# Second layer's attention: products over 64 instead of 49 rows of the query and key tiles, the spare rows zeroed

## What is computed

```python
xn = _layernorm(x, axis=-1)
x = x + _L0_attn_ref(xn, ...) + _L0_ffn_ref(xn, ...)
xn = _layernorm(x, axis=-1)
x = x + _L1_attn_ref(xn, ...) + _L1_ffn_ref(xn, ...)
```

```python
q = rope(heads(x @ W_q.T + b_q))
k = rope(heads(x @ W_k.T + b_k))
v = heads(x @ W_v.T + b_v)
scores = jnp.einsum('bhtd,bhsd->bhts', q, k)
probs = jax.nn.softmax((scores + mask) / jnp.sqrt(jnp.float32(dh)), axis=-1)
out = jnp.einsum('bhts,bhsd->bhtd', probs, v)
out = out.transpose(0, 2, 1, 3).reshape(b, t, d)
return out @ W_o.T + b_o
```

## Time and profile before

| | us |
|---|---|
| median of 3 runs | 2048.22 |
| lowest, highest | 2047.69, 2049.31 |
| the profiled execution | 2053.99 |
| its span, first to last instruction | 2052.1 |
| PE busy in it | 1683.1 (82%) |
| DVE busy | 1229.1 (60%) |
| ACT busy | 901.6 (44%) |
| mean granted clock of PE | 0.891 |

### The profile page before, as it was taken

The page is one execution under the profiler, slowest core; times in us unless marked ns, Lnnn a source line. Parts: engine busy times, 40 slices in busy tenths (PEclk is TensorE's granted clock), DMA queues, the critical chain, the costliest instruction groups (busy, mean ns, idle before and its releaser), DMA issues. The chain is left out here.

```text
span 2052.1 us, 35695 instructions
## 1 busy us (share of the span) xinstructions
PE 1683.1 (82%) x13083; PEld 838.5 (41%) x13083; DVE 1229.1 (60%) x2140; ACT 901.6 (44%) x1457; POOL 768.6 (37%) x423
## 2 busy tenths in 40 slices
PE   2777798798989988899899972459988889898988
PEld 2455354353544535454353432236633333323333
DVE  5422876758675675766766506811357766676573
ACT  0112265364554635546454540213235655455455
POOL 1502745556475663755657671710035000000000
PEclk9998699899998999999999985679979988798688
DMA  4122200000000000000000001233310000000000
GB/s 155 52 81 85 44 12 11 7 22 7 23 12 13 17 10 21 12 18 12 12 19 7 17 6 57 86 105 103 93 41 23 21 27 27 28 2 27 27 1 21
DMA packets 59157, 69.96 MB, mean 34 GB/s; under 512 B 13274, under 2 KB 42862, under 8 KB 58094
## 3 DMA queue, kind: packets, MB, share of 16 engines
q1 hardware_dynamic: 54894, 59.31, 9.3%
q0 software_dynamic: 4096, 8.40, 1.5%
HBM read 43.48 MB, written 19.53 MB: 31 GB/s over the span
## 5 line engine op out<-in xcount | busy, mean ns | idle before, releaser
L1480 POOL TENSOR_TENSOR a_prob_sum<-a_prob_sum,a_prob 128x1024 f32<-128x1024 f32 (+2 forms) x224 | 499.4, 2230 | 236.4 <-ACT a_prob L1428 215.5
L1428 ACT ACTIVATE a_prob<-a_st,a_table 128x512 f32<-128x512 f32 (+3 forms) x640 | 352.7, 626 | 355.3 <-PE a_st L1306 218.1
L1918 DVE TENSOR_REDUCE a_maxima<-a_mx 128x1 f32<-128x512 f32 (+3 forms) x640 | 351.5, 604 | 148.1 <-PE a_mx L1906 107.7
L1526 DVE TENSOR_REDUCE a_maxima<-a_ring 128x16 f32<-128x512 f32 (+3 forms) x640 | 352.8, 600 | 128.9 <-PE a_ring L1238 101.5
L2175 ACT ACTIVATE a_prob<-a_st 128x1024 f32<-128x1024 f32 (+1 forms) x320 | 271.5, 899 | 228.7 <-PE a_st L2075 130.1
L1333 PE MATMUL a_ot<-a_prob,a_values 128*64 128x512 f32 (+3 forms) x1280 | 287.8, 568 | 0.0
L1238 PE MATMUL a_ring<-a_k_hi,a_q_hi 64*128 64x512 f16 (+3 forms) x640 | 165.3, 374 | 92.0 <-DVE a_maxima L1526 69.2
L1906 PE MATMUL a_mx<-a_ks,a_qs 49*128 49x512 bf16 (+3 forms) x640 | 181.5, 393 | 43.1 <-DVE a_maxima L1918 41.7
L2091 PE MATMUL a_ot<-a_prob,a_values 128*32 128x512 f32 (+3 forms) x1280 | 184.7, 633 | 0.0
L1306 PE MATMUL a_st<-a_q_hi,a_k_hi 64*128 64x512 f16 (+4 forms) x704 | 135.1, 339 | 0.0
L2075 PE MATMUL a_st<-a_qs,a_ks 49*128 49x512 bf16 (+3 forms) x640 | 129.9, 401 | 6.1 <-issue 2.4
(11 more groups left out here) (249 smaller groups left out, 2681.8 us busy)
## 6 DMA issues: line engine op xcount, KB each, us to landing
a_rden<-rden_wide SPq DMA_DIRECT2D x64, 128.0 KB, 2.9
f_w<-in_w SPq DMA_DIRECT2D x28, 256.0 KB, 2.8
expert_in<-zeros SPq DMA_DIRECT2D x5, 1024.0 KB, 9.8
f_rows<-expert_in SPq DMA_DIRECT2D x16, 256.0 KB, 3.3
a_values<-values_all SPq DMA_DIRECT2D x8, 512.0 KB
expert_out<-f_result SPq DMA_DIRECT2D x16, 256.0 KB, 2.4
shared_w<-in_w SPq DMA_DIRECT2D x12, 256.0 KB, 3.0
parts<-p_part_t SPq DMA_DIRECT2D x6, 512.0 KB, 2.7
```

The lines of the kernel that those rows point to most:

```text
L1428: e = act.activation(prob[:, s % NPROB, a, c0:QW], ps_st[s % 2][:, a, c0:QW], ACT.Exp, bias=table[x][:, a, at:at + 1])
L1480: pool.tensor_tensor(into[:, :, c0:QW], into[:, :, c0:QW], here[:, :, c0:QW], ALU.add).then_inc(added, 2 if r == TPQ - 2 else 1)
L1526: dve.reduce_max(maxima[:, qt // TPQ, a, qt % TPQ, at:at + count], bank[:, 0:hi - lo].rearrange("p (w k) -> p w k", k=WINDOW), AX_X).then_ ...
L1918: dve.reduce_max(own.maxima[:, qt // TPQ, a, qt % TPQ, n:n + 1], bank[:, 0:hi - lo], AX_X).then_inc(done, 1)
```

## The change

`ROWS1` becomes 64, so that both products (`scores` and `max_pair1`) run over all 64 rows of a half. So that the 15 rows beyond the data hold zeros, `set_ones1` clears each of the two tiles whole before it writes the ones: two memsets over 128 partitions and, behind each, a wait of the engine for its own memset. It is called once on DVE (buffer 0) and once on POOL (buffer 1). The loads, the masks, the order of the work and the data rows stay as they are.

```diff
-ROWS1 = PRODUCTS1 + 1 + 2 * DH1
+ROWS1 = 64
...
+    own.cleared = [ctx.enter_context(nc.semaphore(f"a1_cleared{x}")) for x in range(2)]
...
 def set_ones1(eng, own, x):
 
     ones_twice = float(np.array([0x3F803F80], np.uint32).view(np.float32)[0])
+    for n, tile in enumerate((own.qs[x], own.ks[x])):
+        eng.memset(tile[:, :].bitcast(F32), 0.0).then_inc(own.cleared[x], 1)
+        eng.wait_ge(own.cleared[x], n + 1)
     for a in range(2):
```

## The result

The changed kernel takes 2016.66 us (median of 4 runs, 2006.47 to 2020.33) against 2047.95 us (4 runs, 2044.33 to 2049.31): ratio 0.984, 95% interval 0.980 to 0.988, 31 us less. Measured again beside later kernels it came out at 0.980 (0.975 to 0.986). Now and then a run is disturbed; one that lies more than 1.5% above the quickest run of its kernel is left out of the ratios and the mean clocks. The forecast was 2049.3 us with a range down to 2044.5. The sign that the prediction named for this, a clock of 0.88 or more there, is plain with 0.94.

A forecast was written before the change was run, and what follows sets the result against it. PE was taken to bound the second attention at half clock, PE with DVE at full. The terms 0 + 0 + 1.1 + 0 = +1.1 us on the median 2048.22 gave 2049.3 us, range 2044.5 to 2056.

The forecast's parts named there:

- The sign that the prediction named for this: Last 527 us: a granted clock of 0.88 or more would prove the forecast wrong and Rival one right.
- The views and the bound: Second attention, 527 us: PE alone paces it at half clock (169 us), DVE and PE together at full clock.
- Part one: Scores and maxima products of the second attention: 64 rows for 49 cost 0 and gain 0; bound 8 ns a product.
- Part two: PE's clock in the second attention: set by recent busy time, so 64 rows change nothing, +0 us.
- Part three: Start of the second layer's experts: two more DVE memsets delay SP's loads and PE, +1.1 us, bounds 0 to 3.0.
- rival two: Second attention's group turns: the shifted start brings one more long dip, 6.1 us, giving 2055.4 us; chance 0.09.
- Part four: Second layer's experts: two more POOL memsets of 0.97 us each, cost 0, hidden; without cover 1.9 us.
- Rival one: Second attention: wider rows raise PE's clock; half the time at half clock saved, 30 us, gives 2019 us; chance 0.12.

## Why the prediction was wrong

**The views and the bound: right.** PE at half clock was the bound of the stage. The price of a microsecond at half was put at 0.36 us from two slots. The change gave 42.1 us for 117 us, or 0.36; the 33-row kernel lost 149.7 us (685.3 - 535.6) for 610 - 174 = 436 us more at half, or 0.34. Nothing was mis-sized here.

**Part one, the cost of a row: right.** The 216/376 ns stayed, and the pairs still stand 0.22 us apart at full clock and 0.43 at half. The 8 ns a product that the range allowed for weren't there.

**Part two, the clock: this step failed.** It read the earlier trace rows well up to a point: a PE busy for 13.46 of 13.65 us at half clock means that busy time isn't what the clock goes by. It was then talked out of the consequence by one stretch of the first layer, where products of 64 rows also stayed at half for 13.65 us. That stretch shows only that 64 rows are not always enough; PE had waited in it (12.06 busy of 13.65). It doesn't show that 64 rows don't do more than 49, which was the question. A fair comparison needs the same work at two row counts, and no trace of before held that. So "0 for this part" had no row behind it, and the 0.12 for the rival leaned on that one stretch. The runs showed in its place: 33, 49, 56 and 64 rows give clocks of 0.56, 0.82 to 0.86, 0.91 and 0.93 to 0.94 in the last stage, and the change took PE's time at half clock in the attention from 174 to 57 us, worth 42 us. The rule that was weighed there, from the Trainium skill ("TensorE: Matmul & The Clock Gate", the section on the HAM clock gate), says that recent busy time sets the clock. If busy is read as the share of time that PE's records cover, the 33-row trace is at odds with it: PE was busy for 271.87 of 279.89 us at half clock. The measurement decides.

**Part three, the start: its own terms were right, what follows them was not seen.** The chain came as worked out: SP's first load 1.04 us late for 1.1, PE's wait ending 0.60 us late for 1.1. The sum carried that to the end as it was, on the ground that nothing there waits for a clock time of its own. But PE's dips in the experts lengthened: with five memsets on DVE the attention begins about 2 us late in the median (175.4 for 173.5 us behind DVE's first memset), and 4.4 us late in the changed kernel's profile. At 49 rows the late start alone was measured at 0.4% (7.6 us, with an interval of 1 to 14), at a mean clock of 0.886 for 0.890. That fits the mechanism of rival two, a shift that lets the dips fall longer, at about the price given there (6.1 us), without showing it. At 64 rows no such loss shows: on POOL or on DVE, the clearing gave the same time. Whether the dips' length depends on the shift itself or on where PE's stalls fall stays open.

**Part four, the memsets on POOL: right,** as far as the rows go: nothing waited for them.

**Rival one was the case,** and its time of 2019 was 2 us off. That closeness is in part luck. It stood for half of the time at half clock and 1.1 us for the start; in the profiles two thirds went (117 of 174 us, worth 42 us), and 4.4 us were lost ahead of the attention. The price of 0.36 us was right on its merits.

**Rival two read the dips too narrowly.** It has one long dip and 13.65 us at the other turns; the kernel before has a second one of 34.13 us. It also took three runs within 1.6 us as a sign that such dips hardly come and go, where 31 runs of this kernel spread over 34 us.

## What to carry to other kernels

Where PE's clock is the bound, a product's empty rows are not free: filled up to its half of the array it took the same time here and kept the clock up (0.94 for 0.83, 1.6 to 2.0% of the whole), with nothing but a one-time clearing of about 2 us to pay. Read a low granted clock under a busy PE as a question about what the products look like, and answer it with a kernel that changes only that; one stretch elsewhere in the trace settles nothing. Added streaming raises the clock too, but costs PE's time and gained nothing here.

## What the runs showed of the hardware

- Rows of a product that hold only zeros or only ones keep the clock as high as each other: ratios 0.980 and 0.982 measured side by side, clock 0.93 in both last stages.
- The effect is graded and steep downwards: 15 rows more gave 1.6 to 2.0%, 16 rows fewer cost 7.6%, with one stretch of 280 us at half clock under a PE busy 97% of it.
- A microsecond of PE at half clock cost 0.36 us in this attention, over twelve profiles with 57 to 202 us of it. That is what the two slots of the earlier trace rows give, 4.21 us at half clock for 2.70 at full.
- At 49 rows two memsets of 0.91 us at the start of the experts came with 0.4 to 0.6% in three measurements (1.0045, 1.0056, 1.0037), more than the 2 us by which the attention begins late. The mean clock is lower by 0.004 to 0.005; how that comes about is open.
- Runs of one and the same kernel differ by more than the first three of before let one think: 2036 to 2070 us over 31 runs, against 2047.69 to 2049.31. In the profiles up to 10.2 us of this have come about before the first instruction that any of the edits touches.
